# GpSimd's gathers of a scan step wait for ScalarE's pieces, three a piece, and row gathers come ahead of value gathers

## What is computed

```python
h = relu(layernorm(x))
wh = (h @ weight).reshape(n, 4, 32)
e = leaky_relu(logit_parent[:, None, :] + logit_child[None, :, :], 0.2)
att = softmax(where(adj[..., None] > 0, e, -9e15), axis=1)
x = x + einsum('njh,jhf->nhf', att, wh)          # first layer
h = relu(layernorm(x))
msg = relu((adj @ h) @ W_msg.T + b_msg)          # second layer
x = x + gru_cell(msg, h, W_ih, W_hh, b_ih, b_hh)
```

## Time and profile before

| | |
|---|---|
| three runs, median | 976.55 us (970.72 to 979.77) |
| the profiled execution, span of the page | 1278.8 us; the page gives no other time of it |
| busy of the span | PE 57%, DVE 58%, ACT 51%, POOL 40% |
| read from HBM, written | 295.65 MB, 12.71 MB |
| mean granted clock of TensorE | 0.746 |

### The profile page before, as it was taken

The page is one execution under the profiler, slowest core; times in us unless marked ns, Lnnn a source line. Parts: engine busy times, 40 slices in busy tenths (PEclk is TensorE's granted clock), DMA queues, the critical chain, the costliest instruction groups (busy, mean ns, idle before and its releaser), DMA issues.

```text
span 1278.8 us, 12294 instructions
## 1 busy us (share of the span) xinstructions
PE 730.5 (57%) x3331; PEld 439.4 (34%) x3381; DVE 744.5 (58%) x3128; ACT 654.5 (51%) x667; POOL 508.6 (40%) x518
## 2 busy tenths in 40 slices
PE   2665447374764747647372726363736454329987
PEld 1443224142432424324141414141414342106643
DVE  7577438484774847748472819383846451127754
ACT  2767518293774937748381809191923122005532
POOL 3110461433426234262435261727255447730360
PEclk9878767685877768777685767676767577659998
DMA  9999928685977969878684858686810002211121
GB/s 318 421 420 423 415 98 344 263 364 209 418 315 297 377 250 415 324 292 349 269 367 145 359 202 334 236 335 233 328 36 19 26 25 51 52 37 34 53 71 34
DMA packets 55750, 305.51 MB, mean 239 GB/s; under 512 B 13825, under 2 KB 31442, under 8 KB 39296
## 3 DMA queue, kind: packets, MB, share of 16 engines
q1 hardware_dynamic: 27936, 274.74, 52.9%
q0 software_dynamic: 17152, 23.15, 6.7%
q10 hardware_dynamic: 10592, 6.82, 1.8%
HBM read 295.65 MB, written 12.71 MB: 241 GB/s over the span
## 4 chain that ended last, share of the span: by engine, by line
another core or an unknown queue 29%; DVE 27%; PE 20%; ACT 11%; issue 8%; DMA 4%; POOL 1%; ACTq 0%; DVEq 0%; POOLq 0%
ACT ind L666 7%; PE ps L925 4%; DVE cand L1389 3%; DVE list_arena L1565 3%; DMA x<-in_x 2%; PE ps L1137 2%; PE ps L970 1%; DVE rows_in L1505 1%; PE ps L971 1%; PE ps L972 1%; PE ps L1160 1%; PE ps L904 1%; PE ps L1162 1%; PE ps L1161 1%
## 5 line engine op out<-in xcount | busy, mean ns | idle before, releaser
L666 ACT ACTIVATE ind<-adj_in 128x4096 bf16<-128x4096 int32 x128 | 461.8, 3608 | 18.1 <-PE ps L925 6.6
L925 PE MATMUL ps<-ind,bit_w 128*128 128x512 bf16 x993 | 318.2, 460 | 194.2 <-ACT ind L666 161.1
L557 POOL DMA_INDIRECT val<-in_adj,val_idx x144 | 151.7, 1054 | 421.7 <-DVE val_idx L1599 351.0
L925 PEld LDWEIGHTS ps<-ind,bit_w 128*128 128x128 bf16 x1024 | 114.5, 114 | 366.5 <-ACT ind L666 175.1
L1389 DVE MAX8 cand<-ps 128x8 f32<-128x256 f32 x256 | 91.1, 418 | 197.2 <-remote 184.3
L539 POOL DMA_INDIRECT rows_in<-wh_table,idx x180 | 180.9, 1005 | 62.3 <-issue 62.3
L617 POOL DMA_INDIRECT adj_in<-g_table,idx x96 | 93.6, 975 | 105.5 <-PE ps L1139 69.3
L694 ACT COPY pm<-ps 128x32 f32<-128x32 f32 x16 | 3.0, 185 | 233.2 <-remote 232.6
L970 PE MATMUL ps<-rows_in,ident 128*128 128x132 f32 x120 | 37.7, 412 | 59.3 <-DVE rows_in L1505 59.2
L957 PE MATMUL ps<-pm,own 128*128 128x8 f32 x128 | 24.5, 320 | 73.0 <-issue 58.9
L1719 DVE TENSOR_SCALAR adj_in<-iota,edge_row,val 128x128 f32<-128x128 f32 x128 | 34.2, 346 | 47.6 <-remote 33.8
(11 more groups left out here) (299 smaller groups left out, 1586.2 us busy)
## 6 DMA issues: line engine op xcount, KB each, us to landing
adj_in<-in_adj SPq DMA_DIRECT2D x128, 2048.0 KB
wh_table<-rows_in POOLq DMA_DIRECT2D x16, 264.0 KB, 8.5
g_table<-t_buf ACTq DMA_DIRECT2D x16, 256.0 KB
out<-rows_in SPq DMA_DIRECT2D x16, 256.0 KB
rows_in<-wh_table,idx POOLq DMA_INDIRECT x180
val<-in_adj,val_idx POOLq DMA_INDIRECT x144
adj_in<-g_table,idx POOLq DMA_INDIRECT x112
ind<-g_table,idx POOLq DMA_INDIRECT x16
```

Source lines behind the costliest of these rows:

```text
L557: nc.gpsimd.indirect_dma_start(out=val2[:, s, k:k + 1], out_offset=None, in_=adj_values, in_offset=bass.IndirectOffsetOnAxis(ap=val_idx2[: ...
L666: nc.scalar.activation(ind[:, (tile * 2 + half) % IND, :], adj_in[:, slot, 0:b - a].bitcast(I32), ACT.Relu, bias=1.0, scale=-1.0, accum_ou ...
L925: ins = nc.tensor.matmul(o, bit_w[:, b, :], ind[:, (tile * 2 + half) % IND, c0:c0 + HALF], start=False, stop=(b == BITS - 1))
```

## The change

A function `beat(s, n)` gives a number of pieces, `2 * G * (s + 1) + 6 + n` with G = 4, and no more than 128. Each triple of gathers in the scan first waits until ScalarE has made that many. The four triples of `rows(s)` wait for pieces 6 and 7 of step s+1, its last one, and the first of step s+2; the three triples of `values(s-1)` for pieces 2, 3 and 4 of step s+2; the two calls of `scan_rows` for its pieces 5 and 6. In the loop `rows(s)` now comes ahead of `values(s-1)`. The calls behind the scan keep their order; the waits in `values(14)` and `values(15)` ask for 128 pieces. No gather is added or taken away, and the other engines' programs are unchanged.

```diff
+                def beat(s, n):
+                    return min(2 * G * (s + 1) + 6 + n, 2 * T)
+
                 def rows(s):
...
                     for t in range(G):
+                        pool.wait_ge(ind_done, beat(s, t))
                         for k in range(3):
...
                 def values(s):
                     pool.wait_ge(idx2_done, s + 1)
                     for k in range(E2):
+                        if k % 3 == 0:
+                            pool.wait_ge(ind_done, beat(s + 1, G + k // 3))
...
                 for s in range(1, NG - 1):
+                    rows(s)
                     values(s - 1)
-                    rows(s)
                     if s == FIRST_SCAN:
                         for par in range(2):
                             pool.wait_ge(g_out[par], 16 * (NG // 4))
                     if 0 <= s - FIRST_SCAN < SCAN_PRE // 2:
+                        pool.wait_ge(ind_done, beat(s, 7))
                         scan_rows(2 * (s - FIRST_SCAN))
+                        pool.wait_ge(ind_done, beat(s, 8))
                         scan_rows(2 * (s - FIRST_SCAN) + 1)
```

## The result

The changed kernel takes 992.90 us (median of 4 runs, 984.42 to 998.96), the kernel before on the same chip 978.16 (4 runs, 970.72 to 982.25): ratio 1.0172 [1.0092, 1.0253]. The ratio is estimated with its interval from the single runs, and isn't quite that of the two medians. On one of the two chips of the experiments the changed kernel gave 995.45 us and 1.0179 [1.0131, 1.0227]. It is slower: by 14.7 us by the two medians, by 1.7% or some 17 us by the ratio, whose interval is 9 to 25 us. The forecast was 987 us, 10.5 us above the 976.55 us it started from.

What follows compares the result with a forecast made beforehand. The prediction took the load of the adjacency matrix as what bounds the scan. 976.55 + 14 (end of the scan) - 3 (bursts) = 987.5, say 987 us, range 982 to 996 at 0.45.

Steps and rivals of the forecast that it cites:

- End of the scan, 14 us: Behind the last pieces GpSimd comes free 13.6 to 15 us later, all reaching the end; 14 us taken as loss.
- GpSimd is never idle: From early_rows(8) behind the scan to the first message row GpSimd has no idle time, so its whole delay counts.
- TensorE bounds the message stage: In the message stage TensorE takes 8.67 us a group, slower than the 6.25 us of five gathers.
- The bursts, -3 us: In the steady scan, spreading each step's 21 gathers gains 3 us, between bounds of 0 and 41.
- The unseen waits: TensorE's waits in or behind gather bursts, some 372 us without a seen releaser, are mostly added by the profiler.
- the span after would be near 1060: The changed kernel's profiled span falls from 1278.8 us to near 1060, nearly all 255 us of scan waits gone.
- T at 713 us: The scan, ending with ScalarE's piece 128, ends at 713 us: 286 MB of loads at 415 GB/s take 689 us.
- the 60 us unassigned: The whole kernel's timed median is 60 us above the 917 us worked out from loads and the stretch behind.
- Rival A: In the scan, bursts hold TensorE in timed runs too, so the change is faster: 963.5 or 936 us; chance 0.22.
- Rival B: Behind the scan GpSimd isn't last and idles before values(15), so the end costs nothing: about 975 us; chance 0.28.
- Rival C: In scan steps the fourth triple of rows is late for child_logits: 28 us would give 1015; chance 0.05.

Runs made afterwards that it cites:

- runs 4 and 5: 4: the change in steps 13 and 14 only, ratio 1.0135; 5: the kernel before with values(13) held until piece 128, ratio 1.0206.
- run 2: The kernel before with rows(s) ahead of values(s-1) and no waits: 983.09 us, ratio 1.0071.
- run 6: The kernel before with early_rows(8) and (9) behind the last values, (10) and (11) in the message stage: 980.13 us, ratio 1.0056.
- run 7: The change in steps 1 to 8 only, the order of before without waits from step 9 on: 973.75 us, ratio 0.9994.
- run 9: The changed kernel with values ahead of rows again, so the waits alone: 1199.91 us, ratio 1.2311.
- run 8: The changed kernel with early_rows(8) and (9) behind the last values, (10) and (11) in the message stage: 987.23 us, ratio 1.0133.
- run 1: The kernel before, unchanged, profiled again: 971.34 us, span 969.5.

## Why the prediction was right, and where it was off

- **End of the scan, 14 us: right.** Forecast were early_rows(8) at T + 13.4 and T + 27.0 and a difference of 13.6 to 15; measured T + 12.0 and T + 28.3, a difference of 16.3, of which 14.2 us reach the first message row. The last row gather ends at T + 10.3, where about 10 were named. Values(13) crossing from ahead of piece 128 to behind it is the cause, and runs 4 and 5 make the same delay with other edits. How much of it is the order's (its 7 us of run 2) and how much the waits' can't be said: in the changed kernel both bring the same gathers behind T.
- **"GpSimd is never idle" to the first message row: off in detail, without effect.** It is idle 5.62 us before and 5.63 after, behind early_rows(11). The path leaves GpSimd at the last value gather and comes back by VectorE, TensorE, ScalarE and a store. Both kernels have it, so the message stage opens 9 to 10 us later than worked out in each (T + 76.5 for 67.4, T + 90.7 for 81), and the difference stays right.
- **TensorE bounds the message stage: right**, 145.7 us in both (823.80 to 969.5, 842.08 to 987.8), and by run 6 GpSimd was close behind it.
- **The bursts, -3 us: wrong.** This was the term that was mis-sized: no gain shows. It rested on one stretch of the earlier trace rows in which three engines stood still, in the message stage; in the second profile TensorE is busy 135 of the 146 us there. In the scan the rate is the same (397 and 396 GB/s), and run 7 with eight paced steps gained 0.6 us with an interval of 4 us either way. By the Trainium skill (SBUF — State Buffer, "SBUF: two separate sides"), which the forecast had weighed, it would have been 0 too; the runs agree in the result, but none of them tests ports.
- **The rest of the difference.** 14 - 3 = 11 were forecast against 14.7 us by the medians and 17 by the ratio. 3 us are the term of the bursts; the rest, 1 to 3 us, is within the noise, or part of the 4 us by which T differs in one pair of profiles. 1.6 us of the distance from 987 to 992.90 us are the median of the kernel before, which a fourth run moved to 978.16. T came out at 747.2 to 748.4 us in four kernels and at 751.4 to 758.5 in six others (run 9 aside), without any order that follows an edit (747.2 was run 8, which has the whole change in its scan; the two latest, 756.5 and 758.5, belong to profiled executions that were the slowest of their kernels' six). Whether the change also delays T by a few us stays open.
- **The unseen waits: half right.** That timed runs don't have them was right, and the median could be forecast for that reason alone. "Something that the profiler adds" was wrong as a rule, and with it the step that the span after would be near 1060: it is 987.8, since the waits behind the scan are gone as well.
- **T at 713 us and the 60 us unassigned.** T is 747, 34 us later. That is the rate, 394 GB/s between 24 and 747 us and not 415. Four stretches of 10 us without gathers moved 432, 407, 419 and 405 GB/s (310, 400, 440 and 530 us), so the 433 of the earlier trace rows was the top and not the rule. The work behind T took 222 us (969.5 - 747.3) instead of 204 (18 us), half of it ahead of the first message row; and the span of this execution lies 7 us below the median. That is the 60, and the second profile has no unseen wait in it.
- **Rival A** (bursts) fell with run 1. **Rival B** (GpSimd not last) needed 14 us of unseen waits on VectorE's side: VectorE's last value indices came at T + 46.7, and GpSimd asked for them at T + 54.0, so the margin was 7 us the other way:

```profile
794.01 0.17 DVE L1599 TENSOR_TENSOR val_idx<-row_i,idx 128x9 int32<-128x9 int32 x1
```

- **Rival C** (late rows) cost 2.0 us in one late step; run 9 shows that its mechanism is real and dear as soon as the rows stand behind the waiting values.

## What to carry to other kernels

Spreading an engine's work by making it wait for another's progress is free only while that engine has idle time left to come back; ahead of a point where its queue runs full to the end, each us of lag is a us of the total, so stop pacing some steps before it (run 7 stopped at step 8 of 14 and cost nothing that could be told, but gained nothing either). With an added wait, follow what is queued behind it round the engines: if it comes back to the producer waited for, the wait is paid in every step. And profile a kernel a second time before explaining waits whose releaser the profile doesn't see, above all when the span is far from the timed median.

## What was not expected of the hardware

- Two profiled executions of the same kernel had spans of 1278.8 and 969.5 us. The longer one had 372 us of waits without a releaser, each in or behind a burst of gathers; eleven later profiles, of this kernel, the changed one and their variants, had none, though this kernel's had the same bursts (21 gathers a step, 96 message gathers in 128 us). What made the waits is open.
- With gathers spread or in bursts, the loads moved the same 396 to 397 GB/s between 190 us and T.
- In the changed kernel the time from the issue of the last value gather to its data was 2.39 us behind the scan, where a stretch moves 32 GB/s, while the median of all 144 value gathers, most of them beside the loads, was 6.1 us.
